# A two-layer transformer on eight cores: a second pair of weight buffers, the top-k search moved into the shared expert, and GpSimd taken out of the joins

## What is computed

```python
logits = einsum('bsd,ed->bse', x, gate_w)
scores = softmax(logits).transpose(0, 2, 1)
topk_w, topk_idx = top_k(scores, 256)                 # per expert
x_tok = take_along_axis(x, topk_idx)
h  = gelu(einsum(x_tok, Wg)) * einsum(x_tok, Wu)      # 256 x 2048 per expert
eo = einsum(h, Wd) * topk_w
out = scatter_add(eo at topk_idx) + shared            # shared: the same form over all tokens
```

## Time and profile before

| | us |
|---|---|
| median of 2 runs | 10,859.9 |
| lowest, highest | 10,807.8, 10,911.9 |
| profiled execution | 10,878.9 |
| its span on the slowest core, core 5 | 10,877.4 |
| its spans on the other cores | 10,791.0 to 10,840.8 |
| PE busy in the span | 5862.6 (54%) |
| DVE, ACT, POOL busy | 1829.0, 2237.1, 227.5 |

### The profile page before, as it was taken

The page is one execution under the profiler, slowest core; times in us unless marked ns, Lnnn a source line. Parts: engine busy times, 40 slices in busy tenths (PEclk is TensorE's granted clock), DMA queues, the critical chain, the costliest instruction groups (busy, mean ns, idle before and its releaser), DMA issues.

```text
span 10877.4 us, 64166 instructions; the slowest of 8 cores (10791.0 to 10877.4 us)
## 1 busy us (share of the span) xinstructions
PE 5862.6 (54%) x23468; PEld 2334.5 (21%) x23468; DVE 1829.0 (17%) x2707; ACT 2237.1 (21%) x3687; POOL 227.5 (2%) x433
## 2 busy tenths in 40 slices
PE   3565555555542664454454555468555555554577
PEld 1331000000131223333333333234100000011223
DVE  3322111111136110010010100321211111113010
ACT  1114333333220000000000000112433333322322
POOL 0000000000000000000000000000000000000000
PEclk5565555555555887777777777756555555556788
DMA  1000000000000334424434334100000000000123
GB/s 38 8 11 8 0 0 0 0 0 0 0 1 16 54 54 79 76 55 77 81 57 79 62 72 75 31 10 14 8 0 0 0 0 0 0 0 11 28 38 79
DMA packets 59581, 306.61 MB, mean 28 GB/s; under 512 B 7536, under 2 KB 7936, under 8 KB 29456
## 3 DMA queue, kind: packets, MB, share of 16 engines
q0 software_dynamic: 57952, 285.67, 14.7%
q1 hardware_dynamic: 1328, 16.84, 0.4%
HBM read 579.65 MB, written 8.39 MB: 54 GB/s over the span
## 4 chain that ended last, share of the span: by engine, by line
PE 52%; ACT 14%; DMA 13%; DVE 12%; issue 6%; DVEq 2%; POOL 0%; ACTq 0%; POOLq 0%; PEldq 0%
ACT arena L644 11%; PE ps L652 10%; PE ps L637 9%; DMA arena<-wu_s 6%; PE ps L514 5%; DMA arena<-wd_s 5%; DVE ps L660 4%; PE ps L1130 3%; PE ps L1262 3%; PE ps L1098 3%; PE ps L1101 3%; PE ps L1042 2%; PE ps L1169 2%; PE ps L1323 2%; DVEq L77 1%
## 5 line engine op out<-in xcount | busy, mean ns | idle before, releaser
L652 PE MATMUL ps<-arena 128*65 128x512 bf16 x2048 | 1059.1, 620 | 1490.4 <-ACT arena L644 1490.4
L644 ACT ACTIVATE arena<-ps,mnegc 128x1024 bf16<-128x1024 f32 x1024 | 1140.8, 1114 | 2246.8 <-PE ps L637 2158.9
L637 PE MATMUL ps<-arena 64*128 64x512 bf16 x2048 | 1055.5, 617 | 1.1 <-ACTq L85 1.1
L660 DVE RECIPROCAL ps<-ps 1x1024 f32<-1x1024 f32 x64 | 419.8, 6560 | 3394.9 <-PE ps L652 3394.9
L1098 PE MATMUL ps<-arena 128*128 128x256 bf16 x2048 | 566.7, 314 | 676.2 <-DMA arena<-wu_s 665.2
L652 PEld LDWEIGHTS ps<-arena 128*65 128x65 bf16 x2048 | 192.3, 143 | 2388.7 <-issue 2388.7
L1130 PE MATMUL ps<-arena 128*128 128x512 bf16 x1024 | 362.8, 532 | 580.7 <-DMA arena<-wd_s 580.7
L514 PE MATMUL ps<-wbuf,arena 128*128 128x256 bf16 x3072 | 628.8, 373 | 47.3 <-DMA rows<-bqkv 47.3
L1101 PE MATMUL ps<-arena 128*128 128x256 bf16 x2048 | 564.1, 313 | 0.0
L514 PEld LDWEIGHTS ps<-wbuf,arena 128*128 128x128 bf16 x3072 | 371.6, 128 | 178.4 <-issue 49.9
L1262 PE MATMUL ps<-arena 128*128 128x512 bf16 x1024 | 333.1, 498 | 111.9 <-ACT arena L1251 111.9
(11 more groups left out here) (175 smaller groups left out, 5172.3 us busy)
## 6 DMA issues: line engine op xcount, KB each, us to landing
arena<-wg_s POOLq DMA_DIRECT2D x64, 1024.0 KB, 7.8
arena<-wu_s POOLq DMA_DIRECT2D x64, 1024.0 KB, 12.2
arena<-wd_s POOLq DMA_DIRECT2D x64, 1024.0 KB, 7.9
arena<-wsd_s POOLq DMA_DIRECT2D x64, 256.0 KB, 3.8
wbuf<-w_s POOLq DMA_DIRECT2D x64, 256.0 KB, 3.8
arena<-w_s POOLq DMA_DIRECT2D x16, 1024.0 KB, 7.7
arena<-wsg_s POOLq DMA_DIRECT2D x8, 1024.0 KB, 8.6
arena<-wsu_s POOLq DMA_DIRECT2D x8, 1024.0 KB, 12.9
```

The lines of the kernel that those rows point to most:

```text
L637: half=half, off=off, qh=qh: e.matmul(pss[:, half * 512:(half + 1) * 512], kt[off:off + 64, ts(kc)], qt[off:off + 64, qh * 1024 + half * 5 ...
L644: etok = b.emit("scalar", lambda e, pss=pss, bp=bp: e.activation(s.p_t[bp][:], pss, AF.Exp, bias=s.mneg_col[:]), inc=s.SS)
L652: ptok = b.emit("tensor", lambda e, kc=kc, h=h, half=half, bp=bp: e.matmul(self.PS[0:DH + 1, 2048 + half * 512:2048 + (half + 1) * 512], s ...
L660: trc = b.emit("vector", lambda e: e.reciprocal(self.PS[0:1, 3072:4096], self.PS[DH:DH + 1, 2048:3072]), inc=s.VS)
```

## The change

1. `join` counts three engines, without GpSimd, and keeps its tokens. A new `gp_fence` makes GpSimd wait for those of the last join. It stands at the start of attention, before the loads of `wout`, at the start of the gate, before the shared expert, before the experts' index constants and at the start of layer 1's feed-forward.
2. The 32 search rounds become `sel_iter`, called once at the head of each of the shared expert's 32 blocks. The tail of the top-k part, with its join, moves behind the shared expert. PE waits for the last two copies of the scores before it goes on to the shared expert.
3. A second pair of buffers, `wsA2` and `wsB2`, in memory that the search and the shared expert have left. The groups of the experts alternate between the pairs, over the ends of experts too; up groups use both buffers of a pair, down groups the first. A load waits for the last group that used the same pair.

```diff
-    def join(self, engines=("tensor", "vector", "scalar", "gpsimd")):
+    def join(self, engines=("tensor", "vector", "scalar")):
...
+        self.last_join = toks
         return toks
+
+    def gp_fence(self):
+        for tok in getattr(self, "last_join", {}).values():
+            self.wait("gpsimd", tok)
...
-        for it in range(CAP // 8):
+        self._sel_left = CAP // 8
+
+        def sel_iter():
+            if self._sel_left <= 0:
+                return
+            self._sel_left -= 1
             b.emit("vector", lambda e: e.max(out=max8[:], in_=s.scores_work[:]))
             b.drain("vector")
             b.emit("vector", lambda e: e.match_replace(
                 out=s.scores_work[:], in_to_replace=max8[:], in_values=s.scores_work[:],
                 imm_value=-1000.0))
             b.drain("vector")
...
+        b.gp_fence()
+        b.wait("tensor", tp_g[2])
+        b.wait("tensor", tp_g[3])
         for th in (1, 0):
...
                 for fsq in range(4):
                     fs = q * 4 + fsq
+                    sel_iter()
...
+        while self._sel_left > 0:
+            sel_iter()
+        tsel = b.emit("vector", lambda e: e.tensor_single_scalar(
+            sel_fm[:], s.scores_work[:], -999.0, ALU.is_lt), inc=s.VS)
...
+        b.join()
...
+        wsA2 = s.av(119808, 128, 4096)
+        wsB2 = s.av(108544, 128, 4096)
+        s.wsp = [(wsA, wsB), (wsA2, wsB2)]
+        s.wsp_sem = [(s.SA, s.SB), (s.SA2, s.SB2)]
+        self._wpair_g = {}
+        self._wgrp = 0
...
         for q in range(4):
-            b.wait("gpsimd", self._wsAB_g)
...
+            p = self._wgrp % 2
+            self._wgrp += 1
+            wA, wB = s.wsp[p]
+            semA, semB = s.wsp_sem[p]
+            b.wait("gpsimd", self._wpair_g.get(p))
...
-            self._wsAB_g = uplast
+            self._wpair_g[p] = uplast
...
         for q in range(4):
-            wq = wsA if q % 2 == 0 else wsB
-            b.wait("gpsimd", self._wsAB_g)
+            p = self._wgrp % 2
+            self._wgrp += 1
+            wq = s.wsp[p][0]
+            b.wait("gpsimd", self._wpair_g.get(p))
...
-            self._wsAB_g = dlast
+            self._wpair_g[p] = dlast
```

More of the change, by code:

```diff
@@ L222, in build @@
             s.SB = b.semaphore("SB")
+            s.SA2 = b.semaphore("SA2")
+            s.SB2 = b.semaphore("SB2")
             s.SD = [b.semaphore("SD0"), b.semaphore("SD1")]
@@ L973, in moe @@
             return
+        while self._sel_left > 0:
+            sel_iter()
+        tsel = b.emit("vector", lambda e: e.tensor_single_scalar(
+            sel_fm[:], s.scores_work[:], -999.0, ALU.is_lt), inc=s.VS)
+        tp_g = {}
+        b.wait("tensor", tsel)
+        for tc in range(TC):
+            tb = 2 + (tc % 2)
+            pt = self.bank(tb, dt=BF16)[0:128, 0:16]
+            b.wait("tensor", tp_g.get(tb))
+            ttk = b.emit("tensor", lambda e, pt=pt, tc=tc: e.transpose(
+                pt, sel_fm[:, ts(tc)], s.ident[0:16, 0:16]), inc=s.TS)
+            b.wait("scalar", ttk)
+            stok = b.emit("scalar", lambda e, pt=pt, tc=tc: e.copy(
+                sel_tm[:, tc * 16:(tc + 1) * 16], pt), inc=s.SS)
+            tp_g[tb] = stok
+            b.wait("tensor", stok)
+        rk_tok = None
+        first = True
+        for tc in range(TC):
+            psr = self.PS[0:128, 4 * 512 + tc * 16: 4 * 512 + (tc + 1) * 16]
+            for c2 in range(tc + 1):
+                lhs = lt_sb[:] if c2 == tc else s.ones[:]
+                last = (tc == TC - 1 and c2 == tc)
+                rk_tok = b.emit("tensor", lambda e, psr=psr, c2=c2, lhs=lhs,
+                                st=first, sp=last: e.matmul(
+                    psr, lhs, sel_tm[:, c2 * 16:(c2 + 1) * 16], start=st, stop=sp),
+                    inc=(s.TS if last else None))
+                first = False
+        b.wait("vector", rk_tok)
+        for tc in range(TC):
+            psr = self.PS[0:128, 4 * 512 + tc * 16: 4 * 512 + (tc + 1) * 16]
+            mk = markers[:, tc * 16:(tc + 1) * 16]
+            sl = sel_tm[:, tc * 16:(tc + 1) * 16]
+            b.emit("vector", lambda e, psr=psr, mk=mk, sl=sl: e.scalar_tensor_tensor(
+                mk, psr, float(CAP), sl, ALU.is_le, ALU.mult))
+            b.drain("vector")
+            b.emit("vector", lambda e, psr=psr, mk=mk: e.tensor_mul(mk, mk, psr))
+            b.drain("vector")
+            b.emit("vector", lambda e, mk=mk: e.tensor_scalar_add(mk, mk, -1.0))
+            b.drain("vector")
+        b.join()
+        if self.upto == "l0r":
+            return
         M_PERM = 0
@@ L1083, in expert @@
         for q in range(4):
-            b.wait("gpsimd", self._wsAB_g)
[L1085 to L1088, removed]
+            p = self._wgrp % 2
[3 more added lines that the diff above has]
+            b.wait("gpsimd", self._wpair_g.get(p))
+            wtA = b.emit("gpsimd", lambda e, q=q, ex=ex, wA=wA: e.dma_start(
+                out=wA[:], in_=dram["wg_s"][ex, q]), inc=semA, by=16)
+            wtB = b.emit("gpsimd", lambda e, q=q, ex=ex, wB=wB: e.dma_start(
+                out=wB[:], in_=dram["wu_s"][ex, q]), inc=semB, by=16)
             b.wait("tensor", wtA)
@@ L1097, in expert @@
                 for dc in range(DC):
-                    b.emit("tensor", lambda e, psg=psg, fsq=fsq, dc=dc: e.matmul(
-                        psg, wsA[:, (fsq * 8 + dc) * 128:(fsq * 8 + dc + 1) * 128],
+                    b.emit("tensor", lambda e, psg=psg, fsq=fsq, dc=dc, wA=wA: e.matmul(
+                        psg, wA[:, (fsq * 8 + dc) * 128:(fsq * 8 + dc + 1) * 128],
                         xtok[dc][:], start=(dc == 0), stop=(dc == DC - 1)))
-                    uplast = b.emit("tensor", lambda e, psu=psu, fsq=fsq, dc=dc: e.matmul(
-                        psu, wsB[:, (fsq * 8 + dc) * 128:(fsq * 8 + dc + 1) * 128],
+                    uplast = b.emit("tensor", lambda e, psu=psu, fsq=fsq, dc=dc, wB=wB: e.matmul(
+                        psu, wB[:, (fsq * 8 + dc) * 128:(fsq * 8 + dc + 1) * 128],
                         xtok[dc][:], start=(dc == 0), stop=(dc == DC - 1)),
@@ L1118, in expert @@
         for q in range(4):
-            wq = wsA if q % 2 == 0 else wsB
-            b.wait("gpsimd", self._wsAB_g)
+            p = self._wgrp % 2
+            self._wgrp += 1
+            wq = s.wsp[p][0]
+            b.wait("gpsimd", self._wpair_g.get(p))
             wt = b.emit("gpsimd", lambda e, q=q, ex=ex, wq=wq: e.dma_start(
                 out=wq[:], in_=dram["wd_s"][ex, q]),
-                inc=(s.SA if q % 2 == 0 else s.SB), by=16)
+                inc=s.wsp_sem[p][0], by=16)
             b.wait("tensor", wt)
```

## The result

| | before | after |
|---|---|---|
| median, us | 10,818.5 (10 runs) | 9,679.2 (11 runs) |
| lowest, highest | 10,797.2, 10,935.6 | 9,669.4, 9,762.4 |
| profiled execution | 10,878.9 | 9,670.4 |
| its span, slowest core | 10,877.4 (core 5) | 9,668.9 (core 6) |

The ratio is 0.894, with a 95% interval of 0.890 to 0.897. Forecast were 9600 us in a range of 9480 to 9790. From profiled execution to profiled execution the time fell by 1208 us, against 1259 in my sum; between the medians it fell by 1139 us.

What follows compares the result with a forecast made beforehand. PE and DMA taking turns in the routed experts bound the kernel; 1075 (experts) + 155 (search) + 29 (GpSimd) = 1259 us off 10,878.9 gave 9620, less 19 for the median 9601, rounded to 9600; range 9480 to 9790.

Steps and rivals of the forecast that it cites:

- my sum: Whole kernel: 1075 us from experts, 155 from search, 29 from GpSimd, together 1259 us off the profiled 10,878.9 us.
- What bounds the kernel: Routed experts: PE and DMA engines take turns; PE waits 665.2 us for wu_s and 580.7 us for wd_s.
- The steps through one expert: Routed experts: eight weight groups timed from issue to end, groups counted from 0; 69.6 us against 136.8, gain 1075 us.
- the prediction's other estimate: Expert loads: by the Trainium skill's bandwidth rule, 5.9 us per tile at worst, gain some 1050 us.
- The neighbour rival: Expert loads: neighbouring core always takes its share, 7.0 us per tile, gain 941 + 184 us, 9735 us; chance 0.15.
- The search: Top-k rounds moved into the shared expert: first shared matmul 190 us sooner, tail 28 us back, net 155 us.
- The 7 us of PE waiting for DVE: Shared expert: search rounds make a multiplication 0.3 us late in 24 of 32 blocks, 7 us in all.
- GpSimd's part: Joins without GpSimd: loads run ahead in the shared expert and last stage, joins need no answer; 29 us.
- The clock: PE's granted clock of 0.81 becomes the bound, costing 8 x 16 us and 40 in the shared expert, 9770 us; chance 0.10.
- Better than counted: Routed experts: six tiles pass back to back after group 0, 57.4 us per expert, 9410 us; chance 0.08.
- No help: Routed experts: the second buffer pair doesn't help, only 184 us gained, 10,680 us, within 2%; chance 0.03.
- slower: Routed experts: tiles in flight slow each other, phase longer than before, over 2% slower from 162 us per expert; chance 0.01.

Runs made afterwards that it cites:

- e_pairs: The second pair of expert weight buffers alone, on the kernel before; 9883.3 us, ratio 0.910.
- e_join: GpSimd out of the joins, with the fences, alone on the kernel before; ratio 0.999 (0.996 to 1.002).
- e_again: The whole change run once more, unaltered, beside another version on one chip; 9750.3 us, ratio 0.896.
- e_ring: Whole change plus down groups in both buffers, down group 0 loaded early into attention's buffers, up groups halved in four slots; 9429.2 us, again 9397.6 us.
- e_early: Whole change plus down groups in both buffers of a pair and down group 0 loaded early into attention's weight buffers; 9485.6 us, ratio 0.874.

## Why the prediction was right, and what it missed

**What bounds the kernel: right.** Waits of 1246 us were the gain to be had, 341 stayed (forecast: near 300), and e_pairs shows that nothing else in the experts moved.

**The steps through one expert: right in order, 3.7 us short in size.** The times at which the queue issues a group's loads give the ends of the groups. From the end of group 1 on, the steps had 17.5, 8.0, 5.4, 8.7, 5.1 and 9.0 us; measured means over fifteen experts of core 6 were 17.6, 10.3, 5.0, 10.6, 4.8 and 9.9. On the six cores whose records are complete the phase is 72.6 us. The groups' own durations make 50.9 of it, against 50.7 in the steps; that is luck in part, for group 2 took 9.2 us where I had 10.2, and the second and fourth down groups 5.5 where I had 4.7. The excess is in the waits ahead of the groups, 21.8 us against 18.9.

So the mis-sized term is the time from the end of one group to the start of the one whose load was issued then. For group 2's pair it was 15.2 us over the cores (13.6 before, 14.3 in the steps). The first down group's tile was still on its way when the second's was issued, and that one took 10.3 us instead of 9.4; the fourth's took 9.2. The spacing of tiles in the queue was right: group 3's pair landed 11.1 us after group 2's over the cores (11.5 on core 6), against 2 x 5.6. But group 2, shorter than I had it, covered less of that, and PE waited for group 3 1.8 us on average and not 1.0.

Why a load takes longer than before can be read in pairs of cores. Core 6 while core 7 is quiet, then while both load; then the same two windows of core 7:

```profile
5118.00:5134.00 16.00, 6.61 (x21) 2.74 (x23) 4.29 (x16) 2.12 (x2) 2.15 (x4) 0.68 1.04 217
5172.00:5178.00 6.00, 2.44 (x12) 1.75 (x13) 0.00 (x0) 0.00 (x0) 0.00 (x0) 0.50 1.04 164
```

```profile
5118.00:5134.00 16.00, 14.71 (x209) 13.17 (x207) 1.69 (x4) 3.11 (x11) 1.05 (x2) 1.00 0.01 2
5172.00:5178.00 6.00, 2.39 (x6) 0.87 (x7) 0.00 (x0) 0.00 (x0) 0.00 (x0) 0.66 1.01 156
```

1.05 MB at 217 GB/s is 4.8 us, at 164 it is 6.4 and at 156 6.7, more than the 5.9 us that the prediction's other estimate had at worst. The DMA engines are shown as fully busy either way. The change raises the loading share from 38% to 59%, so the neighbour is met more often. The neighbour rival had 134 us less gain than the forecast; the experts' stage gave 61 less. How much of the 61 is the neighbour's isn't shown. Phases that are longer come in pairs of cores: 4 and 5 in the kernel before, and in e_join cores 2 and 3 (136.2 and 136.6 us) and 6 and 7 (138.6 and 138.0), where the others have 132.3 to 132.9. Most of the excess is waiting for loads: 80 us per expert on cores 6 and 7, 74 to 75 on the four quick ones. No run silences a neighbour, since all cores run one program; that the two share what slows them is read from such rows.

**The search: right.** 158 us in its stage against 155. The 7 us of PE waiting for DVE aren't there; the first shared matmul came 188 us sooner and not 190, and the stretch from there to the first gather grew by 30 us and not 28. DVE's timeline in a block of the kernel after:

```profile
3296.37 0.69 DVE L868 TENSOR_TENSOR arena<-arena,ps 128x512 bf16<-128x512 bf16 x1 [1.49 <-ACT arena L865]
3296.97 2.27 DVE L825 MAX8 arena<-arena 16x8 f32<-16x2048 f32 x1
...
3299.40 2.26 DVE L827 MATCH_REPLACE8 arena<-arena 16x2048 f32<-16x2048 f32 x1
3301.81 0.69 DVE L868 TENSOR_TENSOR arena<-arena,ps 128x512 bf16<-128x512 bf16 x1
3303.28 0.69 DVE L868 TENSOR_TENSOR arena<-arena,ps 128x512 bf16<-128x512 bf16 x1 [0.78 <-ACT arena L865]
3303.88 2.27 DVE L825 MAX8 arena<-arena 16x8 f32<-16x2048 f32 x1
...
3308.72 0.69 DVE L868 TENSOR_TENSOR arena<-arena,ps 128x512 bf16<-128x512 bf16 x1
```

The order is as predicted: a round begins as a block's last multiplication ends, and the next block's first one comes late. But the round begins 0.1 us before that multiplication's recorded end, the multiplication runs 5.44 us after the last and not 5.50, and the waits of PE for DVE in the first shared matmuls sum up to 1.3 us. A margin of 0.25 us was less than my reading of such rows could carry.

**GpSimd's part: right.** 29 us forecast; 23 from the search to the experts and 4 in the last stage measured, and 16 and 3 when part 1 is alone.

**The sum.** Against the profiled execution: the experts' stage gave 1014 us where I had 1075, the rest 194 where I had 184. Of the 194, 11 are no part of the change: the first search round starts at 3278.1 us after and at 3289.0 before. Together the gain is 51 us less, 9670 for 9620. The median came out 79 us above the forecast: these 51, the 19 that I took off for the median of before, and 9 by which the execution profiled after lies below its median. Against the median of ten runs of the kernel before, 10,818.5 us, the gain is 1139 us and not 1260. The execution that the sum started from lay 60 us above that median, with cores 4 and 5 slow, so a part of its phase of 136.7 us wasn't the kernel's usual time.

**The other rivals.** The clock: it wasn't met in the execution profiled after, where no core was at 0.81 in the experts' stage, but it isn't out. In e_again it came for a part of the stages and cost a phase some 3.4 us where it held, less than half of the 8 us that I had priced, and some 60 us in the last stage, which I hadn't priced. Better than counted: out for the change as it is; e_ring gets below its 57.4 us by issuing earlier, e_early comes to 61.9. No help and slower: out.

## What to carry to other kernels

A second pair of buffers takes away only what one group of matmuls covers; write down issue, landing and end of each group before, and the groups that are shorter than a load's latency show themselves as the next stall. When they do, more bytes in flight earlier (the idle half of a pair, buffers of a stage that is over, half groups) brought another 302 us here by phases and 353 between the medians of one chip. Price a transfer at the rate it gets while the neighbouring core loads too, in the share of time that the change will give it.

## What the runs showed of the hardware

- Two neighbouring cores that load at once got 164 and 156 GB/s written (bf16 from float32 in memory, so twice that read), one alone 217. In the kernel before, cores 4 and 5 had 199 and 149.
- With loads off, PE of one core kept full clock for 21 us of dense matmuls and 0.91 over 300 us, while in the output projection of layer 0 it had 0.81 over 16 us before the change and 1.00 in the same window of e_again (core 5 both times):

```profile
2952.00:2968.00 16.00, 16.00 (x76) 7.28 (x75) 6.86 (x10) 0.00 (x0) 0.00 (x0) 1.00 0.00 1
```

  What decides between the two isn't shown by these runs.
- The clock of 0.81 came to neighbouring cores together, while all eight ran the same work. In e_again, from 5250 to 5640 us the mean clock was 0.72 to 0.73 on cores 2, 3, 6 and 7 and 0.84 to 0.86 on 0, 1, 4 and 5; in the last stage it was the other way round, 0.71 to 0.74 on cores 0, 1, 4 and 5 and 0.81 to 0.82 on the rest (8850 to 9700 us), and that stage took 946 to 955 us instead of 892 to 896.
- Behind 96 matmuls of one column the clock fell: in the kernel before it was at 0.50 from 1 us into the dense group that follows them, with no gap over 0.8 us in between the earlier trace rows. That these matmuls are the cause isn't shown.
